# More attention chunks transposed in 32 x 32 blocks, with their DMAs split in two, and one pair of additions moved

## What is computed

```
theta_x = einsum('ld,bdt->btl', theta_w, context) + theta_b
phi_x   = einsum('ld,bdt->blt', phi_w, layernorm(x)) + phi_b
p       = softmax(einsum('btl,bls->bts', theta_x, phi_x), axis=-1)     # 512 x 512 for each batch
g_x     = einsum('ld,bdt->btl', g_w, layernorm(x)) + g_b
t_x     = einsum('bts,bsl->blt', p, g_x)                               # needs p with s on the partitions
h       = relu(normalise t_x over (l, t), * gamma + beta)
x       = x + tanh(gate) * (out_w h + out_b + context)
x       = x + tanh(gate2) * bitlinear feed-forward(layernorm(x))
```

## Time and profile before

| | |
|---|---|
| median of 3 runs | 297.95 us (297.81 to 297.99) |
| the profiled execution's own time | 298.51 us |
| its span | 296.7 us |
| PE busy | 290.8 us, 98% |
| DVE busy | 239.7 us, 81% |
| ACT busy | 195.5 us, 66% |
| POOL busy | 198.3 us, 67% |
| granted TensorE clock, mean | 0.999 |

### The profile page before, as it was taken

One profiled execution on the slowest core, in us unless ns is written; L12 is line 12 of the kernel. 1 busy time (PEld: TensorE's weight loads), 2 busy tenths in 40 slices (PEclk: granted clock), 3 DMA queues, 4 the chain that ended last, 5 costly groups with the idle time before them and its releaser, 6 DMA issues.

```text
span 296.7 us, 4393 instructions
## 1 busy us (share of the span) xinstructions
PE 290.8 (98%) x1310; PEld 155.9 (53%) x1310; DVE 239.7 (81%) x539; ACT 195.5 (66%) x319; POOL 198.3 (67%) x302
## 2 busy tenths in 40 slices
PE   8999999999999999999999999999999999999996
PEld 6766756575757565544444444444444444444444
DVE  3796977989898786999889787986986896867872
ACT  2387987989898898799765645465456456345620
POOL 3362598959593958657798777686786786655710
PEclk9999999999999999999999999999999999999999
DMA  7999596849494001010335474334343362641355
GB/s 238 408 418 411 227 325 259 263 147 344 155 345 146 0 2 35 1 39 0 71 71 59 88 142 106 61 82 106 72 96 84 75 103 72 131 116 29 83 100 180
DMA packets 56535, 42.23 MB, mean 142 GB/s; under 512 B 43456, under 2 KB 46656, under 8 KB 55488
## 3 DMA queue, kind: packets, MB, share of 16 engines
q1 hardware_dynamic: 56224, 41.69, 48.8%
q10 hardware_dynamic: 288, 0.27, 0.3%
HBM read 24.65 MB, written 6.82 MB: 106 GB/s over the span
## 4 chain that ended last, share of the span: by engine, by line
PE 79%; DVE 6%; POOL 4%; issue 3%; DMA 3%; ACT 2%; SPq 1%; POOLq 0%; DVEq 0%
PE bank L1240 37%; PE bank L1258 14%; PE bank L1184 8%; PE bank L1156 5%; PE bank L1201 4%; PE bank L1171 3%; PE bank L1133 2%; PE bank L1120 2%; DMA x<-x_dram 2%; PE bank L1143 2%; POOL stage L401 1%; PE bank L1271 1%; DMA probT<-prob 1%; POOL prob L385 1%; DVE xst L725 1%
## 5 line engine op out<-in xcount | busy, mean ns | idle before, releaser
L1240 PE MATMUL bank<-wq,stage 128*128 128x512 bf16 x512 | 113.3, 379 | 0.0
L1240 PEld LDWEIGHTS bank<-wq,stage 128*128 128x128 bf16 x512 | 50.1, 98 | 61.5 <-issue 2.3
L872 DVE SCALAR_TENSOR_TENSOR stage<-bank,s,stage 128x512 f32<-128x512 f32 x64 | 47.6, 744 | 22.6 <-PE bank L1240 18.6
L615 ACT ACTIVATE xn<-stage 128x1024 f32<-128x1024 f32 x31 | 32.8, 1057 | 46.1 <-DVE stage L872 46.1
L607 ACT ACTIVATE stage<-bank,s 128x512 f32<-128x512 f32 x64 | 43.1, 680 | 16.5 <-PE bank L1240 14.4
L1258 PE MATMUL bank<-wq,prob 128*128 128x512 bf16 x224 | 50.5, 379 | 0.0
L467 POOL TENSOR_SCALAR stage<-stage,hsc 128x1024 f32<-128x1024 f32 x30 | 33.3, 1119 | 20.6 <-DVE hsc L903 20.6
L877 DVE TENSOR_REDUCE m<-stage 128x1 f32<-128x1024 f32 x31 | 37.7, 1215 | 0.8
L1258 PEld LDWEIGHTS bank<-wq,prob 128*128 128x128 bf16 x224 | 21.9, 98 | 26.4
L1156 PE MATMUL bank<-ph,th 128*128 128x512 f32 x96 | 34.4, 471 | 0.3 <-DVE ph L753 0.3
L473 POOL TENSOR_SCALAR prob<-stage 128x1024 bf16<-128x1024 f32 x30 | 30.8, 1044 | 0.0
(11 more groups left out here) (122 smaller groups left out, 460.9 us busy)
## 6 DMA issues: line engine op xcount, KB each, us to landing
stage<-w1t_dram SPq DMA_DIRECT2D x4, 1024.0 KB, 12.1
stage<-w2t_dram SPq DMA_DIRECT2D x4, 1024.0 KB, 9.1
stage<-w3t_dram SPq DMA_DIRECT2D x4, 1024.0 KB, 6.5
x<-x_dram SPq DMA_DIRECT2D x7, 512.0 KB, 8.6
c_sb<-ctx_in_dram SPq DMA_DIRECT2D x7, 512.0 KB, 6.8
out_dram<-stage SPq DMA_DIRECT2D x14, 256.0 KB, 2.4
spill<-blocks SPq DMA_DIRECT2D x5, 512.0 KB, 2.6
placed<-spill SPq DMA_DIRECT2D x20, 128.0 KB, 2.8
```

Of the source, the lines that this page charges most:

```text
L615: A.activation(junk, h_sb[t % 2][:, half * HF:(half + 1) * HF], ACT.Square, accum_out=ssq[:, half:half + 1]).then_inc(sq_done, 1)
L872: V.scalar_tensor_tensor(h_sb[k][:, c * 512:(c + 1) * 512], up_banks(n)[1][:, :], s12[:, u % 2, 1, k:k + 1], sil[n % 3], ALU.mult, ALU.mul ...
L1240: last = mm(bank[:, :], turned[:, row:row + P], wq[:, at:at + 512], start=q == 0, stop=q == KI - 1)
```

## The change

For batches 2 to 5, chunk 1 also goes by blocks, so that three chunks do and PE turns only chunk 0. Batch 6 now goes by blocks for chunks 2 and 3, and its values for them stand at the end of PE's step 7. The DMAs carry 768 KB instead of 512 KB for batches 2 to 5; `move_blocks` is split in `send_blocks` and `fetch_blocks`, a weight load stands between the two for batch 4, and a sixth pair is added for batch 6. In step 7 `residual` stands behind row_max 3. With batch 6 by blocks, ACT normalises two of its chunks and POOL the other two.

```diff
-        blocks = sb("blocks", [P, TC * 2 * P])
-        placed = sb("placed", [P, 4, 2 * P])
+        blocks = sb("blocks", [P, TC * 3 * P])
+        placed = sb("placed", [P, TC * 3 * P])
...
+        def first_block(i):
+            return 2 if i in (1, B - 2) else 1 if 2 <= i <= B - 3 else TC
         def by_blocks(i):
-            return 1 <= i <= B - 3
+            return first_block(i) < TC
...
-            def move_blocks(i):
-                sp.wait_ge(blocks_ready, 2 * i)
+            def send_blocks(i):
+                n = TC - first_block(i)
+                sp.wait_ge(blocks_ready, block_no(i))
                 if i >= 2:
                     sp.wait_ge(blocks_moved, 64 * (i - 1))
-                sp.dma_start(spill[:, :], blocks[:, :]).then_inc(blocks_out, 16)
+                sp.dma_start(spill[:, 0:TC * n * P], blocks[:, 0:TC * n * P]).then_inc(blocks_out, 16)
+            def fetch_blocks(i):
+                n = TC - first_block(i)
                 sp.wait_ge(blocks_out, 16 * i)
                 sp.wait_ge(tx_done, i)
                 for k in range(4):
-                    sp.dma_start(placed[32 * k:32 * (k + 1)], spill_v[k]).then_inc(blocks_moved, 16)
+                    back = spill[:, k * n * P:(k + 1) * n * P].rearrange("(q b) r -> b q r", b=32)
+                    sp.dma_start(placed[32 * k:32 * (k + 1), 0:TC * n * P].rearrange("b (q r) -> b q r", q=4), back)\
+                        .then_inc(blocks_moved, 16)
...
-            move_blocks(4)
+            send_blocks(4)
             load_weight(2, 2)
+            fetch_blocks(4)
             load_c(7)
             load_weight(2, 3)
-            move_blocks(5)
+            send_blocks(5)
+            fetch_blocks(5)
+            send_blocks(6)
+            fetch_blocks(6)
...
-                    p_copy(i - 1, 0)
-                    p_copy(i - 1, 1)
+                    for c in range(min(first_block(i - 1), 2)):
+                        p_copy(i - 1, c)
...
-                if by_blocks(i - 1):
-                    turn_blocks(i - 1, 0)
-                    turn_blocks(i - 1, 1)
+                for c in range(first_block(i - 1), TC):
+                    turn_blocks(i - 1, c)
...
                 tx_var(i - 2)
-                residual(i)
+                if i < 7:
+                    residual(i)
                 row_max(i, 1)
                 tx_norm(i - 2)
                 row_max(i, 2)
                 row_max(i, 3)
+                if i == 7:
+                    residual(i)
...
-                if by_blocks(i - 2):
-                    values(i - 2, 2)
-                    values(i - 2, 3)
+                if i >= 2:
+                    for c in range(first_block(i - 2), TC):
+                        values(i - 2, c)
...
-                if i >= 1:
+                if i >= 1 and first_block(i - 1) > 1:
                     turn_p(i - 1, 1)
...
-                elif i >= 1:
+                elif i >= 1 and first_block(i - 1) > 1:
                     values(i - 1, 1)
                 scores(i, 3)
                 if whole:
                     values(i - 1, 3)
+                elif i == B - 1:
+                    values(i - 1, 2)
+                    values(i - 1, 3)
```

More of the change, by code:

```diff
@@ L78, in gated_cross_attention_bitffn @@
         probT = sb("probT", [P, 2, T])
-        blocks = sb("blocks", [P, TC * 2 * P])
-        placed = sb("placed", [P, 4, 2 * P])
-        spill = nc.dram_tensor("spill", [P, TC * 2 * P], F32, kind="Internal").ap()
-        spill_v = spill.rearrange("(q b) (k r) -> k b q r", b=32, k=4)
+        blocks = sb("blocks", [P, TC * 3 * P])
+        placed = sb("placed", [P, TC * 3 * P])
+        spill = nc.dram_tensor("spill", [P, TC * 3 * P], F32, kind="Internal").ap()
         hn = sb("hn", [P, T])
@@ L153, in b_turn, with block_no @@
             return banks[2] if (i, c) == (B - 1, 2) else banks[4] if i == B - 1 and c == 3 else b_pt[c % 2]
+        def first_block(i):
+            return 2 if i in (1, B - 2) else 1 if 2 <= i <= B - 3 else TC
         def by_blocks(i):
-            return 1 <= i <= B - 3
+            return first_block(i) < TC
         def turn_no(i, c):
-            return c + (2 * i + 2 if by_blocks(i) else 0 if i == 0 else 2 * (B - 3) + 4 * (i - (B - 3)))
+            return c + sum(first_block(j) for j in range(i))
+        def block_no(i):
+            return sum(TC - first_block(j) for j in range(i + 1))
         def turned_p(i, c):
-            if by_blocks(i) and c >= 2:
-                return placed[:, :, (c - 2) * P:(c - 1) * P].rearrange("s q (c r) -> s q c r", c=TC)
+            if c >= first_block(i):
+                n = TC - first_block(i)
+                return placed[:, 0:TC * n * P].rearrange("s (q k c r) -> s k q c r", q=4, k=n, c=TC)[:, c - first_block(i)]
             return c_sb[:, 0, 0] if (i, c) == (B - 1, 2) else probT[:, 0] if i == B - 1 and c == 3 else probT[:, c % 2]
@@ L279, in _ @@
             load_x(4)
-            move_blocks(1)
+            send_blocks(1)
+            fetch_blocks(1)
             load_weight(1, 2)
@@ L284, in _ @@
             load_c(4)
-            move_blocks(2)
+            send_blocks(2)
+            fetch_blocks(2)
             load_x(6)
@@ L288, in _ @@
             load_c(5)
-            move_blocks(3)
+            send_blocks(3)
+            fetch_blocks(3)
             load_weight(2, 0)
@@ L461, in quant_h @@
                 if t < 2:
-                    pool.wait_ge(pT_done, turn_no(B - 2 + t, TC))
+                    pool.wait_ge(pT_done, turn_no(B - 1 + t, 0))
+                    pool.wait_ge(blocks_ready, block_no(B - 2))
                 pool.wait_ge(qs_ready, t + 1)
@@ L764, in sum_inverse, with turn_blocks @@
                 V.reciprocal(rsum[:, :], esum[:, :]).then_inc(rsum_ready, 1)
-            def turn_blocks(i, k):
-                if k == 0:
+            def turn_blocks(i, c):
+                n = TC - first_block(i)
+                if c == first_block(i):
                     dve.wait_ge(pnorm_ready, 4 * i + 4)
@@ L771, in turn_blocks @@
                         dve.wait_ge(blocks_out, 16 * (i - 1))
-                V.transpose(blocks[:, :].rearrange("p (s k c r) -> p k c s r", s=4, k=2, c=TC)[:, k],
-                            prob[:, i % 2, :, (2 + k) * P:(3 + k) * P].rearrange("p c (s r) -> p c s r", r=32))\
+                V.transpose(blocks[:, 0:TC * n * P].rearrange("p (s k c r) -> p k c s r", s=4, k=n, c=TC)[:, c - first_block(i)],
+                            prob[:, i % 2, :, c * P:(c + 1) * P].rearrange("p c (s r) -> p c s r", r=32))\
                     .then_inc(blocks_ready, 1)
@@ L946, in third_step @@
                 low_part(2, th, b_th, 0, th_ready, thl_ready)
-                turn_blocks(1, 0)
-                turn_blocks(1, 1)
+                for c in range(first_block(1), TC):
+                    turn_blocks(1, c)
                 low_part(2, ph, b_ph, 1, ph_ready, phl_ready)
```

## The result

The changed kernel takes 299.42 us (median of 11 runs, 298.24 to 304.78) against 297.82 us for the kernel before (11 runs, 297.71 to 297.99): ratio 1.0044, 95% interval 1.0033 to 1.0056. It is slower by 1.3 us where 0.8 us of gain was forecast. The ratio and the 1.3 us are taken over the fast runs alone, without the two longest executions (304.62 and 304.78); the bare medians lie 1.6 apart. Over all 11 runs the means lie 2.3 us apart. The time also spreads more from run to run than before, which turns out to be part of the answer. Further down too, a ratio need not be the quotient of the two medians beside it (e6: 1.0081, the medians give 1.0066).

What follows compares the result with a forecast made beforehand. PE, busy 98% of the span, was taken to bound the kernel. Terms -2.69 + 0.61 + 0.85 (step 7 idle) + 0.45 (POOL) gave -0.8 us; taken off the median, this made 297.15 us, range 296.2 to 298.1.

Steps and rivals of the forecast that it cites:

- What PE loses: Batches 2 to 5 lose one turn_p each (0.44 us), batch 6 two (0.93): 2.69 us less PE work.
- Step 3: At mean_mm, a third DVE transpose for batch 2 lies wholly on PE's path: 0.61 us lost, M3 at 49.64.
- Hand-offs: Steps 3 to 6: phi's slack falls from 1.46 to 0.16 us, but no stall; the steps stay PE's.
- rival B: Hand-offs taken as free cost 0.15 us in each of steps 4 to 7: 297.75 us, chance 0.24.
- Three-chunk moves: A 768 KB send and fetch takes 8.6 us (bounds 7.2 and 10.8); blocks of batches 3 and 4 arrive in time.
- The upper bound: All of a 512 KB move's 7.2 us scaled by 1.5: 10.8 us; with a weight load, batch 4 is 3.4 late.
- Rival C: Fetch of batch 4, behind the weight load, is 2.2 us late in step 6: 299.35 us, chance 0.1.
- Step 7: Idle time at var_mm and values(6, 0) together grows from 0.55 to 1.4 us, ending near 110.2.
- I let the two cancel: POOL, step 7: moved additions take 0.4 us off tx_root and put as much on prep_root(1) and the roundings.
- Rival A: POOL isn't last at turn_p(7, 0), so the gain is 1.2 us: 296.75 us, chance 0.2.
- Rival D: Waits of step 7 are shorter than worked out, gain 1.8 us: 296.15 us, chance 0.08.
- The second half: From turn_p(7, 0) on all engines follow a dense PE, so the 0.8 us gain reaches the end.

Runs made afterwards that it cites:

- e6: Kernel before with three chunks by blocks (768 KB) for batches 2 to 5, batch 6 and the additions of batch 7 left as before; 300.13 us, 1.0081.
- e2: Changed kernel with the fetch of batch 4 put back ahead of the weight load; 298.56 us, 1.0027.
- e0: Changed kernel unchanged, run again for a second profile (span 298.7 us); 300.02 us, 1.0076, on another chip.
- e4: Changed kernel with batches 2 to 5 back at two chunks and the fetch of batch 4 ahead of the weight load; 298.62 us, 1.0018.
- e5: As e4, with the additions of batch 7 back in their place ahead of row_max 1; 298.43 us, 1.0007.
- e7: Kernel before with one edit, the additions of batch 7 behind row_max 3; 298.39 us, 1.0009.
- e9: Kernel before with three chunks by blocks for batch 3 alone; 297.95 us, 0.9997.
- e11: As e4, with the two additions of batch 7 cut to one column each (output differs); 298.04 us, 0.9992.
- e12: Kernel before with only a quarter of each load of w3 (output differs), the control of e8; 298.16 us, 1.0003.
- e14: Kernel before with the four loads of w3 issued on ACT's queue, the control of e13; 298.92 us, 1.0029.
- e10: Kernel before with three chunks by blocks for batch 6, batches 2 to 5 kept at two; 298.89 us, 1.0029.
- e16: As e6, with ACT taking the signs of w2 ahead of the two sums over w3 in step 6; 297.67 us, 0.9983.
- e13: As e6, with the four loads of w3 issued by ACT instead of SP, in steps 4 and 5; 304.43 us, 1.0221.
- e3: Changed kernel with each 768 KB send made as two DMAs and the fetch of batch 4 ahead of the weight load; 299.48 us, 1.0037.
- e8: As e6, with only a quarter of each load of w3 (output differs); 296.75 us, 0.9958.
- e15: As e2, with the four loads of w3 on ACT's queue; 305.90 us, 1.0264.

## Why the prediction was wrong

It said 297.15 (296.2 to 298.1). Point by point:

- **What PE loses** held. Steps of 13.97 us, M6 to M7 14.20 for 14.19. M6 at 91.92 in e2, for 91.89, is luck: M3 is 0.52 earlier than forecast, and M3 to M4 take 14.85 instead of 14.31, with 0.32 of waiting for batch 2 in it. In step 7 PE's work fell by 0.62, where 0.93 was forecast.
- **Step 3** held as a mechanism: idle 0.71 at mean_mm, less than 1.23. The other half microsecond came off ahead of it: POOL's tx_root(0) took 0.93 where it took 1.53 in the profile before, with the same code. First before, then e0:

```profile
36.75 1.53 POOL L353 TENSOR_TENSOR tsc<-tsc,neghalf 128x1 f32<-128x1 f32 x1 [0.54 <-DVE tsc L794]
```
```profile
36.92 0.93 POOL L374 TENSOR_TENSOR tsc<-tsc,neghalf 128x1 f32<-128x1 f32 x1 [0.54 <-DVE tsc L817]
```

Of the kernels with two chunks for batch 2, e4, e5, e7, e9, e11, e12 and e14 have 0.92 or 0.93 there and no idle time at M3, and e10 has 1.53 and 0.61 of it. So the earlier trace rows's 0.62 was a matter of how two instructions met in that execution. From the small matmul in step 2 to M3 it is 15.42 to 15.44 us in the seven and 16.05 in e0: the third transpose costs its 0.6.
- **Hand-offs** held: no idle time at phi or theta in e0, and rival B falls. e16 alone has 0.43 at theta once.
- **Three-chunk moves** is the step that failed. "512 KB go out in 2.64 us", and 8.6 for a move of 768 KB, were read off a row whose queue was empty, and each move was costed by itself. The sum put nothing for late blocks. Sends took 3.3 to 5.5 us in the changed kernel, 7.84 at worst in e16. The move of batch 4, taken at 8.6 to 8.9 us with the weight load, took 11.8 in e0 (sent at 76.34, PE released at 88.18) and 14.7 in the execution profiled first (75.97 to 90.64). Its rows in e0:

```profile
76.34 0.34 SPq L262 DMA_DIRECT2D spill<-blocks  x1
80.48 1.75 SPq L271 DMA_DIRECT2D placed<-spill  x4
```

PE waited 0.86 for batch 2 and 1.46 for batch 4. Of the 3.1 us by which turn_p(7, 0) in e0 (122.30) is behind the forecast (119.2), 2.5 are there at M7 and 0.6 come in step 7. The upper bound, 10.8 us for all of a move, scaled the bytes and left out what stands ahead of a send (the 2.8 us added to it for batch 4 are the weight load behind the send). The numbers to see it were in the earlier trace rows: a DMA share of 0.73 to 0.74 over a step, whose free part was partly wait for completion, so that 1 us was free where 1.7 was added and the step made 0.44 shorter.
- **Rival C** (chance 0.1, 299.35) named the place, PE waiting for batch 4 in step 6, and came close to the median. The number is luck: C had batch 4 alone late, by 2.2 us, where e0 has batches 2 and 4 late and a loss in step 7. And its mechanism was half of it: with the weight load moved away (e2, e6) batch 4 is in time, and ACT is late for the weights.
- **Step 7.** Idle time at var_mm and values(6, 0) was 0.68 + 0.38 = 1.06 where 1.4 was forecast: right and even better. "I let the two cancel" failed: the additions took 0.37 off tx_root and prep_root(1) took 1.2 longer, 0.8 of it by the additions (e11). Rival A falls with it: POOL is last at turn_p(7, 0). Rival D had these waits a whole microsecond shorter than worked out, and they are 0.3 shorter.
- The second half did follow PE, and turn_x(0) cost nothing that shows in PE's idle times.

Open: what makes the queue's backlog so different from run to run of one program (e16 from 296.31 to 300.24), and the tail of a send with it, isn't shown. The estimate of 15.2 us against 13.97 says that a backlog must come, and not how large it is: behind e10's 3.31 a send of batch 5 took 0.15 us more in e0 and 4.5 more in e16. Whether the loads of w3 could be spread so that three chunks pay every time wasn't tried beyond e13 and e16.

## What to carry to other kernels

Cost a transfer against its queue, not by itself: add up for one step all that the queue carries, from the first issue until the engines are idle, and compare with the step after the change. A duration read where the queue is empty holds only as long as it stays empty, and a change that shortens the step eats that margin from the other side. When a fix moves the wait to the next in the queue (e2, e3, e16), look at the queue as a whole: here only fewer bytes in it (e8) brought the full gain, and an order in which the waiting engine has other work first (e16) brought it in some executions.

## What the runs showed of the hardware

- A fetch of 768 KB in SP's queue took 12.0 us instead of some 5.5, with three loads of 1 MB in ACT's queue, two issued ahead of it and one behind it (e13).
- Long idle times of PE cost more than themselves: behind 5.29 us (e13) and 4.29 us of waiting, six matmuls took 4.54 us instead of 2.84, and behind 5.31 us (e15) 5.34. The granted clock in e13 was 0.97 from 76 to 77 us, 0.50 from 77 to 80 (the lower level, 1.2 GHz), 0.83 in the next microsecond and 1.00 after it (2.4 GHz). Behind 1.46 us in e0 they took 2.84, against 2.74 where nothing was waited for.
- GpSimd instructions on 128x2 values took 0.19 to 0.20 us alone and 0.65 to 0.75 beside VectorE operations with two SBUF inputs; the 0.70 of the root became 1.02 (e0, e4).
- The reads of `placed`, rows of 1.5 KB in DRAM, ran at 215 to 226 GB/s with the engines' share at 1.06 to 1.13 (e0, 83 to 87 us), while weight loads ran near 400.
